# Four common products to the head of up 1, and the rests of B on VectorE

## The reference

```python
h  = x @ wi.T                                    # 256 -> 1024
h += ALPHA * (x @ common_wi_a.T) @ common_wi_b.T
h += ALPHA * (x @ experts_wi_a[e].T) @ experts_wi_b[e].T     # e: expert of the sequence
h  = relu(h)
o  = h @ wo.T                                    # 1024 -> 256
o += ALPHA * (h @ common_wo_a.T) @ common_wo_b.T
o += ALPHA * (h @ experts_wo_a[e].T) @ experts_wo_b[e].T
out = x + o
```

## Time and profile before

| | before |
|---|---|
| median of 3 runs | 129.07 us (128.68 to 130.74) |
| profiled execution, its own time | 129.6 us |
| its span, first to last instruction | 127.5 us |
| busy: TensorE, VectorE, ScalarE, GpSimd | 115.6, 53.0, 45.3, 41.4 us |
| mean granted TensorE clock, share of full | 0.973 |
| moved by DMA | 15.03 MB |

### The profile page before, as it was taken

How to read it: one execution, slowest core, us unless ns; L and a number is a source line. 1 busy time by engine, 2 the same in 40 slices (tenths; PEclk the granted TensorE clock), 3 DMA queues, 4 the chain that set the end, 5 groups by cost and what they waited for, 6 DMA issues and landing times.

```text
span 127.5 us, 1945 instructions
## 1 busy us (share of the span) xinstructions
PE 115.6 (91%) x724; PEld 105.6 (83%) x724; DVE 53.0 (42%) x96; ACT 45.3 (36%) x93; POOL 41.4 (32%) x62
## 2 busy tenths in 40 slices
PE   6899969999910999999999999999999999999971
PEld 6678759888800999998888999988889999999960
DVE  0583897427899414112444442133445111111111
ACT  4545688316691023112366341132335011111120
POOL 2056827998958002020647200625100020200000
PEclk9999999999996579999999999999999999999999
DMA  2999899993480000511500002111400001111112
GB/s 102 370 379 319 313 295 286 404 410 135 124 334 0 0 0 8 206 41 44 171 35 5 0 0 84 63 46 44 162 0 0 0 18 41 34 37 40 41 41 82
DMA packets 7755, 15.03 MB, mean 118 GB/s; under 512 B 866, under 2 KB 4194, under 8 KB 7746
## 3 DMA queue, kind: packets, MB, share of 16 engines
q1 hardware_dynamic: 7026, 13.60, 30.9%
q10 hardware_dynamic: 720, 1.31, 2.9%
HBM read 12.81 MB, written 2.10 MB: 117 GB/s over the span
## 4 chain that ended last, share of the span: by engine, by line
PE 77%; DVE 7%; DMA 6%; issue 4%; SPq 2%; ACT 2%
PE bank_o L622 40%; PE bank_h L541 25%; DMA b_raw<-in_rec_b 5%; PE bank_h L573 4%; PE bank_low L586 2%; PE bank_o L641 2%; DVE hid L420 2%; DVE b_stack L436 1%; DMA idt<-in_ids 1%; DVE xT L425 1%; PE bank_o L541 1%; DVE w_raw L458 1%; PE bank_o L632 1%; SPq L184 1%; ACT b_stack L335 1%
## 5 line engine op out<-in xcount | busy, mean ns | idle before, releaser
L622 PE MATMUL bank_o<-wcat,hid 128*128 128x272 f32 x384 | 53.7, 298 | 5.8 <-DVE hid L420 5.8
L622 PEld LDWEIGHTS bank_o<-wcat,hid 128*128 128x128 f32 x384 | 51.8, 197 | 5.9 <-issue 5.9
L541 PE MATMUL bank_h<-xT,wiT 128*128 128x512 f32 x168 | 42.7, 397 | 1.4 <-DVE hid L420 1.0
L541 PEld LDWEIGHTS bank_h<-xT,wiT 128*128 128x128 f32 x168 | 30.3, 190 | 7.7 <-DVE hid L420 1.2
L420 DVE SCALAR_TENSOR_TENSOR hid<-bank_h,hid 128x512 fp32r<-128x512 f32 x28 | 18.9, 688 | 17.1 <-ACT hid L347 17.1
L347 ACT ACTIVATE hid<-bank_h 128x512 fp32r<-128x512 f32 x28 | 16.3, 600 | 23.3 <-PE bank_h L573 23.1
L480 DVE TENSOR_TENSOR o_sb<-bank_o,x_nat 128x256 f32<-128x256 f32 x16 | 6.8, 425 | 34.2 <-PE bank_o L641 34.2
L243 POOL TENSOR_TENSOR b_stack<-b_raw,b_stack 32x1024 fp32r<-32x1024 f32 x6 | 14.3, 2386 | 8.4 <-ACT b_stack L335 8.4
L261 POOL CAST wcat<-a_raw 128x128 fp32r<-128x128 f32 x8 | 2.5, 314 | 35.1 <-PE bank_o L622 35.0
L359 ACT ACTIVATE rank_sb<-bank_o 128x64 fp32r<-128x64 f32 x16 | 3.6, 223 | 25.2 <-PE bank_o L622 25.2
L367 ACT CAST rank_stack<-bank_o 96x128 fp32r<-96x128 f32 x16 | 4.2, 261 | 20.4 <-PE bank_o L632 20.4
(11 more groups left out here) (39 smaller groups left out, 75.4 us busy)
## 6 DMA issues: line engine op xcount, KB each, us to landing
b_raw<-in_rec_b SPq DMA_DIRECT2D x8, 640.0 KB, 6.4
x_nat<-in_x_n SPq DMA_DIRECT2D x4, 512.0 KB, 6.9
out<-o_sb SPq DMA_DIRECT2D x16, 128.0 KB, 1.7
x_raw<-in_x_t SPq DMA_DIRECT2D x6, 256.0 KB, 3.7
w_raw<-in_wo_t SPq DMA_DIRECT2D x4, 256.0 KB, 9.5
w_raw<-in_wi_t ACTq DMA_DIRECT2D x3, 256.0 KB, 4.4
a_raw<-in_rec_a SPq DMA_DIRECT2D x8, 96.0 KB, 2.7
x_raw<-in_x_t ACTq DMA_DIRECT2D x2, 256.0 KB, 3.3
```

The costliest lines, as they stand in the source:

```text
L541: nc.tensor.matmul(up_bank(q, m)[:, :], wiT_at(sw, k, m), xT[q % 2][sx][:, k, :], start=start, stop=False)
L622: last = nc.tensor.matmul(bank_o[g % NO][:, 0:WIN], hid[q % 2][sh][:, m, tok], wcat[sw][:, m, win], start=(m == 0 and i == 0), stop=(m == ...
```

## The change

Four things are done.

1. The common data. `common` is now 16 rows, sent three times onto partitions 0, 32 and 64 of a `common_raw` that VectorE has cleared (a new memset), and SP issues these three transfers ahead of the B records of step 0. GpSimd's `split_common` moves up to stand right behind `split_a(0)`, and VectorE's `common_b` ahead of the rests of B of step 0.
2. The banks. Tile 7 of up 0 uses bank_low, the ranks of step 1 go into bank_h0, and the tiles of up 1 are dealt anew, so that bank_o1 and bank_o2 are free for products earlier.
3. Up 1. TensorE makes products 0 and 1 after its first main and products 2 and 3 after the first LoRA product. VectorE's sums and rests of wo and ScalarE's casts of it stand at the head of their parts of up 1.
4. B. The rests of steps 1 to 3 move from GpSimd to VectorE, each behind a hidden rest (`hidden_lo`). The bo columns become a record and a transfer of their own (`rec_bo`, `load_bo`, 96x256 each), and the B record shrinks to 1024 columns.

```diff
         def up_bank(q, m):
             if q == 0:
-                return (bank_h + bank_o)[m % 7]
+                return (bank_h + bank_o + [bank_low])[m]
             if q == 1:
-                return [bank_h[1], bank_h[2], bank_h[3], bank_h[0], bank_o[0], bank_h[1], bank_h[2], bank_h[3]][m]
+                return [bank_h[1], bank_h[2], bank_h[3], bank_o[0], bank_low, bank_h[0], bank_h[1], bank_h[2]][m]
             return bank_h[m % 4]
+
+        def ranks_bank(q):
+            return bank_h[0] if q == 1 else bank_low
 
         def up_bank_free(q, m):
             if q == 0:
-                return 1 if m == 7 else 0
+                return 0
             if q == 1:
-                return [2, 3, 4, 8, 5, MF + 1, MF + 2, MF + 3][m]
+                return [2, 3, 4, 5, MF, 1, MF + 1, MF + 2][m]
...
+            def load_bo(q):
+                if q >= 2:
+                    sp.wait_ge(bo_ready, (q - 1) * PAIR)
+                for b in range(PAIR):
+                    sp.dma_start(bo_raw[q % 2][:, b, :], rec_bo[bass.ds(expert[q * PAIR + b], 1), :, :].rearrange("o p c -> (o p) c")
+                                 ).then_inc(bo_in[q % 2][b], 16)
...
+            sp.wait_ge(common_zero, 1)
+            for i in range(3):
+                sp.dma_start(common_raw[i * BLK:i * BLK + R, :], common).then_inc(common_in, 16)
             load_b(0)
...
             load_b(1)
-            sp.dma_start(common_raw[:, :], common).then_inc(common_in, 16)
...
             split_a(0)
             pool.wait_ge(a_ready, PAIR)
-            split_bo(0)
+            split_common()
+            pool.wait_ge(common_a_lo, 1)
             split_a(1)
             pool.wait_ge(a_ready, 2 * PAIR)
-            split_b_lo(1, 0)
-            split_b_lo(1, 1)
-            pool.wait_ge(b_lo[1], PAIR)
-            split_common()
-            pool.wait_ge(common_a_lo, 1)
             copy_ao(0, 0)
             copy_ao(0, 1)
             pool.wait_ge(ao_ready[1], 1)
+            split_bo(0)
             split_bo(1)
-            split_b_lo(2, 0)
-            split_b_lo(2, 1)
-            pool.wait_ge(b_lo[0], 2 * PAIR)
             split_a(2)
...
             nc.vector.memset(zeros[:, :], 0.0).then_inc(zeros_ready, 1)
+            nc.vector.memset(common_raw[:, :], 0.0).then_inc(common_zero, 1)
...
                 for i in range(1, PIECES):
                     split_wi_lo(i)
+                common_b()
                 split_b_lo(0, 0)
...
                 for m in range(MF):
                     hidden_lo(0, m)
+                    if m in (4, 6):
+                        split_b_lo(1, m // 2 - 2)
                 ranks_in_lo(1)
 
             def up(q):
+                if q == 1:
+                    for part in (wo_part_sum, wo_part_lo):
+                        part(0)
+                        part(1)
                 for m in range(MF):
                     hidden_lo(q, m)
                     if q == 1 and m == 0:
-                        common_b()
-                    if q == 1 and m >= 3 and m < 7:
-                        wo_part_sum(m - 3)
-                    if q == 1 and m >= 4:
-                        wo_part_lo(m - 4)
+                        for part in (wo_part_sum, wo_part_lo):
+                            part(2)
+                            part(3)
+                    if q == 1 and m in (4, 5):
+                        split_b_lo(2, m - 4)
+                    if q == 2 and m in (3, 5):
+                        split_b_lo(3, m // 2 - 1)
...
             def wo_product(i):
                 if i == 0:
                     pe.wait_ge(common_a_lo, 1)
                     pe.wait_ge(common_b_lo, 1)
-                    pe.wait_ge(hid_lo, MF)
-                if i >= 2:
+                if i < 2:
+                    pe.wait_ge(hid_lo, 6 + i)
+                else:
                     pe.wait_ge(wo_sum, i - 1)
...
                     if g == 0:
-                        pe.wait_ge(hid_lo, MF + 5)
-                        pe.wait_ge(wo_sum, PIECES)
+                        pe.wait_ge(hid_lo, MF + 4)
```

More of the change, by code:

```diff
@@ L15, with conditional_ffn @@
 STAGES = [("up", 0), ("up", 1), ("down", 0), ("up", 2), ("down", 1), ("up", 3), ("down", 2), ("down", 3)]
-def conditional_ffn(nc, x_t, x_n, ids, wi_t, wo_t, rec_a, rec_b, common, out):
+def conditional_ffn(nc, x_t, x_n, ids, wi_t, wo_t, rec_a, rec_b, rec_bo, common, out):
     P = 128
@@ L340, in ranks_in_hi @@
                     act.wait_ge(up_done, (q - 1) * MF)
-                nc.scalar.mul(low_stack[q % 2][:, :], bank_low[:, :], ALPHA).then_inc(low_hi, 1)
+                nc.scalar.mul(low_stack[q % 2][:, :], ranks_bank(q)[:, :], ALPHA).then_inc(low_hi, 1)
             def hidden_hi(q, m):
@@ L441, in ranks_in_lo @@
                 rows = low_stack[q % 2][LOW_LO:LOW_LO + BLK, :]
-                lo_part(rows, bank_low[LOW_LO:LOW_LO + BLK, :], ALPHA, rows).then_inc(low_lo, 1)
+                lo_part(rows, ranks_bank(q)[LOW_LO:LOW_LO + BLK, :], ALPHA, rows).then_inc(low_lo, 1)
             def hidden_lo(q, m):
@@ L585, in ranks_in @@
                     for s in (HI, LO):
-                        last = nc.tensor.matmul(bank_low[:, cols], a_stack[q % 2][:, b, k, :], xT[q % 2][s][:, k, cols],
+                        last = nc.tensor.matmul(ranks_bank(q)[:, cols], a_stack[q % 2][:, b, k, :], xT[q % 2][s][:, k, cols],
                                                 start=(k == 0 and s == HI), stop=(k == KD - 1 and s == LO))
@@ L657, in first_up @@
                 up_main(0, 7)
-                for m in range(4, 7):
+                for m in range(4, MF):
                     up_lora(0, m)
```

99 lines of the change are left out of this document (49 added, 50 removed).

## The result

The changed kernel takes 125.4 us (median of 4 runs, 124.28 to 126.33), the kernel before took 129.35 us beside it: a ratio of 0.968 with an interval of 0.958 to 0.979. It is faster by some 4 us; the forecast was 123.4, 2.0 us less. In its profiled execution it took 126.3 us with a span of 124.5.

What follows compares the result with a forecast made beforehand. TensorE, 91% busy, bounds the kernel; only its waits and low clock can be gained. Down 0 3.3 us earlier plus 2.4 us clock: 129.6 - 5.7 = 123.9, less 0.5 for the runs' median, 123.4; own range 122.5 to 124.6, wide 121.3 to 126.4.

Steps and rivals of the forecast that it cites:

- rival 1: Clock falls in up 1, where TensorE pauses five times between 22.4 and 28.0; costs 2.42 us, giving 125.8; chance 0.13.
- Rival 2: Pause moves to the head: locks on VectorE's SBUF rests give TensorE 2.8 us of waits, 126.2; chance 0.11.
- Products at the head: Common products early in up 1: the 5.8 us pause goes, down 0 starts at 37.9 instead of 41.20, 3.3 us.
- the clock: Down 0 after the pause: without the fall to 0.50, 36 matmuls take 4.53 instead of 6.95 us; 2.4 us gained.
- GpSimd's lock on the first B rests: split_common locks VectorE out till 13.5 in step 0; low_lo at 16.65 instead of 15.73, plus 0.9 us.
- Up 0 with eight banks: Product of m = 7 in up 0 uses bank_low and no longer waits for a hidden rest; 1.0 us gone.
- Waits of up 1: New TensorE waits for hidden rests, low_lo and sums in up 1: 0.65, 0.4, 1.1, 0.4, 0.4; sum 2.95 us.
- Common data to the front of SP's queue: Head of DMA queue: B's cast stays, common lands 3.8 us after issue; a skill-page estimate would add 0.5 us.
- B's rests of steps 2 and 3: Moved to VectorE among hidden rests: 7.3 us of work fits into 13 us, so they cost nothing.
- Rival 3: Smaller waits: no lock at 13.5 (0.9) and half the up 1 waits gone (1.0), giving 121.5; chance 0.10.
- rival 5: Change does not do what it says: down 0 still waits on wo, about 127; chance 0.06.
- Rival 4: Common lands late at the head, at 16.0, 6.0 us late; with the clock's 2.4 us, 131.8; chance 0.04.

Runs made afterwards that it cites:

- Experiment 4: Changed kernel with the four common products, their sums, casts and wo rests back at the end of up 1; 131.9 us, ratio 1.018 to the kernel before.
- experiment 1: The changed kernel run again without any edit, for a second profile; 126.9 us, ratio 0.976 to the kernel before.
- Experiment 9: experiment 8 with only the three common transfers put back ahead of B of step 0, GpSimd and VectorE order kept; 124.2 us.
- experiment 2: Changed kernel with common's transfers, GpSimd's split and VectorE's common_b moved back behind step 1's A and x work; 123.95 us, ratio 0.956 to the kernel before.
- experiment 7: experiment 2 plus TensorE making mains 0, 1 and 2 of up 1 before the first products; 121.0 us, ratio 0.938 to the kernel before.
- experiment 8: experiment 7 with B's rests of step 1 on GpSimd behind split_common instead of on VectorE; 120.7 us, ratio 0.935 to the kernel before.
- experiment 10: experiment 8 with B's rests of steps 2 and 3 on GpSimd too; 120.65 us, ratio 0.932 to the kernel before.
- experiment 11: experiment 8 run again without any edit; 120.7 us, ratio 0.932 to the kernel before.
- experiment 3: Changed kernel with common sent as one 96-row transfer of 480 KB at the head, no memset; 125.7 us, ratio 0.970 to the kernel before.
- experiment 5: Changed kernel with B's rests of step 1 back on GpSimd instead of VectorE; 123.0 us, ratio 0.954 to the kernel before.

## Why the prediction was right in kind and 2.0 us short

The mechanism held: the pause ahead of down 0 and its echo in the clock are gone, and every later stage runs as before. The 125.4 us lie inside the wide range of 121.3 to 126.4 and outside the forecast's own, 122.5 to 124.6. The time alone would fit the prices of rivals 1 and 2 (125.8 and 126.2), but the profiles show neither of the two as the cause of the 2.0 us; that the number fell into the range they had opened is in part luck. What the steps were worth:

- *Products at the head* and *the clock*: right. Experiment 4 takes only this part away, and both return, the pause as 3.5 us in two pieces inside down 0. The clock's 2.4 us came as forecast (86.3 to 83.9 us behind the start of down 0).
- *GpSimd's lock on the first B rests*: right. L443 took 3.94 and 4.15 us for two where 2.49 is its time undisturbed; low_lo came at 16.63 against 16.65 in the execution whose transfers went well. The second operation of VectorE's common_b, priced under 0.7 us, took 1.17 and 1.19 beside GpSimd's cast; it still fitted into the gap.
- *Up 0 with eight banks*: right, no wait of L558 for a hidden rest is left.
- *Waits of up 1*: 2.95 forecast; counted from start to start as in the walk they are 3.5 us in the profile after and 3.4 in that of experiment 1. The five pieces of the first are 1.22, 0.36, 0.96, 0.49 and 0.46 us against 0.65, 0.4, 1.1, 0.4 and 0.4: only the wait of product 0 was mis-sized by more than 0.15, by some 0.5 us (its 1.13 in experiment 1). It is why TensorE's first matmul of down 0 starts at 38.40 in the timeline (38.56 in the chain) instead of 37.9 even in the good execution.
- ***Common data to the front of SP's queue* is the term that was mis-sized.** The step said that B's cast "stays", since the bytes ahead of it are the same, and took 3.8 us for common by "same place and same size". The bytes are the same, the rate is not: 158 to 245 GB/s from 7.5 to 10.5 us in all eight profiles with common at the head, instead of 338 to 383 in the six without it. A and B land late by up to 2 us, differently in each execution (low_stack's first rest at 15.94, 16.69 and 17.96 in three profiles of one kernel, against the walk's 16.0). The prediction had set itself marks for being wrong: low_stack beyond 17.5, which one profile of three is, and common's landing over 5 us, which two of three are with their last transfer (6.2 and 5.2). The third, a granted clock of 0.50, is in none of the three. Since all behind is one chain, down 0 starts at 38.56, 39.30 and 40.63 by the same amounts. Experiment 9 shows that the place of the transfers alone is enough; in experiments 2, 7, 8, 10 and 11, without them at the head, low_stack's first rest comes at 13.1 to 13.9 in every profile. The Trainium skill (SBUF — State Buffer, section "Door 1: The DMA port swizzle") has a transfer onto 16 partitions at 104 GB/s, and the estimate from it was 0.5 us. The trace is near that rate in the slowest stretch, 107 to 123 GB/s from 7.5 to 8.5 us in the profile after and that of experiment 1. The sign of the loss agrees as well, its size is 0 to 2 us by execution, up to four times the estimate.
- *The clock in up 1*, rival 1: not in the three profiles of the changed kernel, seen once, in that of experiment 2 at 0.57, behind waits of 1.16 and 1.25 us. In experiments 3 and 5 the clock fell earlier, in up 0, behind the 2.2 and 1.9 us that TensorE waited for a late low_stack. No trace shows which of the two is behind the four executions of the changed kernel with a mean clock of 0.986: experiment 2's profiled execution and experiment 3's both have that mean. The second is a result of common at the head, so it adds to the mis-sized term. Experiments 7, 8, 10 and 11, in which TensorE waits little or not at all for either, have no mean below 0.99.
- *B's rests of steps 2 and 3*: nothing, as forecast (experiment 10). *Those of step 1* are the price that the walk named; experiment 5 sizes it at 2 us in this kernel, and experiment 8 at 0.2 once mains cover it.
- *Rival 2* (2.8 us more waits from the head) came at 0.5 us, the wait of product 0. *Rival 3* (smaller waits) and *rival 5* (down 0 still waits) did not come. *Rival 4* came in a small form: common late, and A and B with it.

What stays open is why transfers of common slow the queue. The slow stretch went with them to three places (7.5 to 10.5 us, 13 to 14 in experiments 2, 7, 8, 10 and 11, and 17 to 21 before the change), so it is theirs and not the place's. Both of their forms reach fewer partitions, 16 or 96, than the 128 of B; no run sent common onto 128 or another 240 KB to the head, so form and content are not told apart. Nor does a trace show why A and wi, issued ahead of common, are caught by it in some executions and not in others.

## What to carry to other kernels

Put small data that is needed late behind the data that the first products wait for, even where its bytes seem to cost nothing, and look at GB/s beside the DMA share in several executions. When a product is moved up to end a late pause, count what the engine that feeds it must do first, and put work that is ready (here two more mains) ahead of it; with an undisturbed head that turned 4 us of gain into over 8. A walk with the trace's durations was good to 0.7 us over 38, but only for an execution whose transfers land as assumed, so a landing time needs a range of its own.
